# Router logits of a mixture-of-experts stage, with the tokens as the stationary operand

## The reference

```python
def _L3_ffn_ref(x, gate_w, w_gate, w_up, w_down, sw_gate, sw_up, sw_down):
    b, l, d = x.shape                                  # E, H, K = 16, 128, 8
    xf = x.reshape(-1, d)
    logits = _l2norm(xf) @ _l2norm(gate_w).T
    scores = jax.nn.sigmoid(logits)
    topk_scores, topk_idx = jax.lax.top_k(scores, K)
    topk_w = topk_scores / jnp.sum(topk_scores, axis=-1, keepdims=True)
    combine = jnp.sum(jax.nn.one_hot(topk_idx, E, dtype=xf.dtype) * topk_w[..., None], axis=1)
    g = jnp.einsum('nd,edh->neh', xf, w_gate)
    u = jnp.einsum('nd,edh->neh', xf, w_up)
    y = jnp.einsum('neh,ehd->ned', jax.nn.silu(g) * u, w_down)
    routed = jnp.einsum('ned,ne->nd', y, combine)
    shared = jax.nn.silu(xf @ sw_gate) * (xf @ sw_up) @ sw_down
    return (routed + shared).reshape(b, l, d)
...
x = x + jnp.tanh(g_ffn[3]) * _L3_ffn_ref(_layernorm(x, axis=-1), ...)
```

## Time and profile before

| | |
|---|---|
| times of three runs | 1162.62, 1164.57, 1879.65 us |
| median | 1164.57 us |
| time of the profiled execution | 1164.86 us |
| its span, first to last instruction | 1163.1 us |
| mean granted clock of PE | 0.963 |
| busy over the span | PE 1059.1 us (91%), DVE 796.5 (68%), ACT 517.9 (45%), POOL 165.6 (14%) |

### The profile page before, as it was taken

The page is one execution under the profiler, slowest core; times in us unless marked ns, Lnnn a source line. Parts: engine busy times, 40 slices in busy tenths (PEclk is TensorE's granted clock), DMA queues, the critical chain, the costliest instruction groups (busy, mean ns, idle before and its releaser), DMA issues.

```text
span 1163.1 us, 18686 instructions
## 1 busy us (share of the span) xinstructions
PE 1059.1 (91%) x6180; PEld 906.3 (78%) x6180; DVE 796.5 (68%) x1816; ACT 517.9 (45%) x1190; POOL 165.6 (14%) x224
## 2 busy tenths in 40 slices
PE   4775799998899969997999997999969999999998
PEld 3664467776899948886888886999848888888887
DVE  5597889976788745436888875888547564565544
ACT  2556544432555545444544452566533333333222
POOL 2231000000112043211111001133213000010000
PEclk9988899999999979998999998999979999999999
DMA  9301010001000000000000005000012212121221
GB/s 288 85 1 39 1 11 1 1 1 39 34 1 0 1 12 1 1 1 1 1 1 0 0 1 228 4 0 1 1 49 62 66 51 77 56 73 46 67 83 32
DMA packets 30373, 41.18 MB, mean 35 GB/s; under 512 B 13615, under 2 KB 19577, under 8 KB 29414
## 3 DMA queue, kind: packets, MB, share of 16 engines
q1 hardware_dynamic: 29437, 39.63, 11.1%
q10 hardware_dynamic: 873, 0.72, 0.3%
HBM read 37.80 MB, written 2.54 MB: 35 GB/s over the span
## 4 chain that ended last, share of the span: by engine, by line
PE 82%; DVE 9%; ACT 4%; issue 2%; DMA 2%; SPq 1%; POOL 1%; DVEq 0%; POOLq 0%; ACTq 0%
PE psum L1919 15%; PE psum L1929 8%; PE psum L1518 7%; PE psum L336 6%; PE psum L1328 6%; PE psum L1151 6%; PE psum L1109 5%; PE psum L1306 5%; PE psum L1732 4%; PE psum L1526 4%; PE psum L1719 3%; PE psum L1122 2%; PE psum L1133 2%; PE psum L1316 2%; PE psum L552 1%
## 5 line engine op out<-in xcount | busy, mean ns | idle before, releaser
L298 POOL TENSOR_TENSOR rstd<-ve,mhalf 128x1 f32<-128x1 f32 x128 | 81.3, 635 | 748.8 <-DVE ve L293 748.8
L347 ACT COPY work<-psum 128x256 f32<-128x256 f32 (+1 forms) x240 | 99.0, 437 | 148.4 <-PE psum L336 146.0
L336 PE MATMUL psum<-ident,work 128*128 128x128 f32 (+1 forms) x624 | 104.0, 291 | 33.1 <-DMA ctx<-in_ctx_r 8.9
L336 PEld LDWEIGHTS psum<-ident,work 128*128 128x128 f32 (+1 forms) x624 | 78.4, 151 | 48.0 <-issue 9.1
L2052 DVE TENSOR_TENSOR work<-psum,work 128x512 f32<-128x512 f32 x68 | 46.9, 690 | 88.3 <-ACT work L1989 88.1
L1992 ACT CAST h_hi<-work 128x512 fp32r<-128x512 f32 x68 | 42.2, 621 | 112.1 <-DVE work L2057 101.7
L1518 PE MATMUL psum<-early,work 128*128 128x352 f32 x256 | 84.1, 485 | 6.7 <-ACT zone L480 4.0
L1919 PE MATMUL psum<-x_hi,ew_hi 128*128 128x512 f32 (+1 forms) x272 | 87.1, 402 | 2.6 <-ACT work L1989 2.6
L1919 PE MATMUL psum<-x_lo,ew_hi 128*128 128x512 f32 (+1 forms) x272 | 85.2, 395 | 0.0
L1919 PE MATMUL psum<-x_hi,ew_lo 128*128 128x512 f32 (+1 forms) x272 | 84.6, 392 | 0.0
L1929 PE MATMUL psum<-ew_hi,h_hi 128*128 128x256 f32 x272 | 76.4, 281 | 4.7 <-DVE x L2072 3.8
(11 more groups left out here) (258 smaller groups left out, 2542.6 us busy)
## 6 DMA issues: line engine op xcount, KB each, us to landing
work<-expert_shares SPq DMA_DIRECT2D x64, 256.0 KB, 3.2
early<-in_experts_in SPq DMA_DIRECT2D x1, 6528.0 KB, 20.0
x<-in_x_in SPq DMA_DIRECT2D x4, 512.0 KB, 7.5
early<-in_W_in SPq DMA_DIRECT2D x2, 1024.0 KB, 6.0
out_x<-x SPq DMA_DIRECT2D x3, 512.0 KB, 4.4
early<-in_Wk SPq DMA_DIRECT2D x1, 1024.0 KB, 6.8
early<-in_Wq SPq DMA_DIRECT2D x1, 1024.0 KB, 9.1
zone<-in_Wv SPq DMA_DIRECT2D x1, 1024.0 KB, 13.6
```

What stands on the lines that cost most here:

```text
L298: pool.tensor_tensor(rstd[:, slot:slot + 1], ve[:, slot:slot + 1], mhalf[:, 0:1], ALU.pow).then_inc(s["rstd_ready"], 1)
L336: last = pe.transpose(dst[0:rows, at:at + n], src, ident[0:n, 0:n])
L347: act.copy(dst, src).then_inc(s["tr_copied"], 1)
```

## The change

The logits are made with the tokens as the stationary operand. For each of the group's four tiles, six products (three of the split times two halves of the width) load 128 columns of `x_hi` or `x_lo` and stream the 16 columns of `gw_hi` or `gw_lo`; the result has the tokens on the partitions, as the ranking wants it. So 24 products of 16 columns take the place of six of 512 columns, and the four transposes of logits, the copy to `lgT` and the tile `lgT` go. ACT copies the result to `lg` at unit 7 in place of unit 9. The first two gate/up units of the stage both stand behind the logits, at units 7 and 8. The count `tr` is six per group, and waits on it are renumbered. The loop over groups 1 and 2 is written out on PE; ACT and DVE keep theirs.

```diff
-        XT_AT, LG_AT, BT_AT, Z_AT, SIG_AT, TOP_AT, CT_AT = range(2, 6), 7, 9, 10, 10, 11, 13
+        XT_AT, LG_AT, Z_AT, SIG_AT, TOP_AT, CT_AT = range(2, 6), 7, 10, 10, 11, 13
+        FIRST_UNITS = (LG_AT, LG_AT + 1)
...
                 if e == LG_AT:
                     pe.wait_ge(s["tr_copied"], tr.n)
-                    cols = bass.ds(g1 * 512, 512)
-                    passes = [(w, a, k) for w, a in ((gw_hi, x_hi), (gw_hi, x_lo), (gw_lo, x_hi)) for k in range(KD)]
-                    for n, (w, a, k) in enumerate(passes):
-                        last = pe.matmul(bank[5][0:NE, :], w[:, k, :], a[:, k, cols], start=n == 0,
-                                         stop=n == len(passes) - 1)
-                    last.then_inc(s["tr_filled"], 1)
-                    tr.up()
-                if e == BT_AT:
-                    pe.wait_ge(s["tr_copied"], tr.n)
-                    settle(pe, tensor_waits_taken)
                     for j in range(GT):
-                        last = pe.transpose(bank[5][:, j * NE:(j + 1) * NE], lgT[:, j * P:(j + 1) * P],
-                                            ident[0:NE, 0:NE])
+                        cols = bass.ds((g1 * GT + j) * P, P)
+                        passes = [(a, w, k) for a, w in three((x_hi, x_lo), (gw_hi, gw_lo)) for k in range(KD)]
+                        for n, (a, w, k) in enumerate(passes):
+                            last = pe.matmul(bank[5][:, j * NE:(j + 1) * NE], a[:, k, cols], w[:, k, :],
+                                             start=j == 0 and n == 0, stop=j == GT - 1 and n == len(passes) - 1,
+                                             skip_group_check=True)
                     last.then_inc(s["tr_filled"], 1)
                     tr.up()
...
             for e in range(NU):
                 side(0, e)
-                if e in (LG_AT, BT_AT):
-                    gate_up(0, (LG_AT, BT_AT).index(e))
+                if e in FIRST_UNITS:
+                    gate_up(0, FIRST_UNITS.index(e))
             group(0, True, True)
-            looped(pe, [(tr, 7)], G - 2, lambda i: group(i + 1, True))
+            for g in range(1, G - 1):
+                group(g, True)
             group(G - 1, False)
...
                 if e == LG_AT:
-                    act.wait_ge(s["tr_filled"], tr.up())
-                    act.copy(lgT, bank[5][0:NE, :]).then_inc(s["tr_copied"], 1)
-                if e == BT_AT:
                     act.wait_ge(s["tr_filled"], tr.up())
                     act.copy(lg, bank[5][:, 0:GT * NE].rearrange("p (a b) -> p a b", a=GT)
                              ).then_inc(s["tr_copied"], 1)
...
-                    dve.wait_ge(s["tr_copied"], 7 * g1 + 6)
+                    dve.wait_ge(s["tr_copied"], 6 * g1 + 5)
...
-                sp.wait_ge(s["tr_copied"], 7 * g + 7)
+                sp.wait_ge(s["tr_copied"], 6 * g + 6)
```

More of the change, by code:

```diff
@@ L392, in flamingo @@
         share = [carve(work, at, (512,)) for _ in range(RING)]
-        lgT = carve(work, at, (512,), F32, NE)
         combT = carve(work, at, (512,), F32, NE)
@@ L2004, in moe_scalar @@
             group(0, True, True)
-            looped(act, [(tr, 7)], G - 2, lambda i: group(i + 1, True))
+            looped(act, [(tr, 6)], G - 2, lambda i: group(i + 1, True))
             group(G - 1, False)
```

## The result

| | before | changed |
|---|---|---|
| median of 6 runs each | 1164.40 us | 1170.11 us |
| lowest and highest | 1162.62 to 1879.65 | 1169.43 to 1173.55 |
| span of the profiled execution | 1163.1 | 1167.7 |
| products of PE in it | 6180 | 6236 |
| mean granted clock | 0.963 | 0.957 |

The ratio is 1.0055, 95% interval 1.0043 to 1.0067: slower by 5.7 us (some 5.0 to 7.8), clear of noise and far within two per cent. The forecast was 1172, from +7.3. The 1879.65 is a single run of the kernel before, 60% above all others of it, and does not enter the ratio.

What follows compares the result with a forecast made beforehand. The prediction took PE's queue to bound the stage's steady part and a chain of waits its start. From 1164.9 us it added 0 (loop), 2.6 (loads), 3.4 (clock) and 1.3 (start) to reach 1172, range 1164 to 1177.

Steps and rivals of the forecast that it cites:

- The written-out loop: PE's loop over groups 1 and 2: writing it out gains nothing, 0, bounds -0.3 and +1 us.
- The loads: Three steady groups: 24 short products cost more than the removed work, +0.86 us per group, +2.6 us (0.6 to 3.3).
- The restart of 0.10: Behind each steady burst: 0.1 us for restarting long products, whose first load has nothing to hide behind.
- the removed 1.92: Steady groups: old logits products (1.38) and their transposes (0.54) cost 1.92 us per group, all on the path.
- the transposes' 0.085: Old logits' transposes, 0.085 us each, taken as the lower bound of a short product's step: +0.2 us per group.
- The clock: Steady bursts: short products often drop PE's clock; two drops in three bursts taken, +3.4 us (0 to 10).
- The start: Start of the MoE stage: PE reaches the combine weights' transposes 1.0 to 1.4 us later, +1.3 us (-0.5 to +1.8).
- The sum: Whole kernel: 1164.9 + 0 + 2.6 + 3.4 + 1.3 = 1172.2 us; median 1172.
- Rival B: Steady bursts: the clock holds, so 1164.9 + 2.6 + 1.3 = 1168.8 us; chance 0.26.

Runs made afterwards that it cites:

- e5: Changed kernel with the combine weights' transposes at the start moved between the gate and up halves of the second unit; ratio 1.0034, median 1168.40 us.
- e4: Changed kernel with each of the 24 products streaming its 16 columns eight times over (128 columns); ratio 1.0029, median 1168.24 us.
- e8: Changed kernel with 128-column streaming and the combine weights' transposes between the halves of unit 1 at the start; ratio 1.0000, median 1166.39 us.
- e3: Changed kernel with each steady burst of 24 short products cut into four of 6 around the down products; ratio 1.0032, median 1167.77 us.
- e7: Changed kernel with each steady short product put behind one long product of units 7 and 8; ratio 1.0072, median 1172.83 us.
- e10: Changed kernel with each steady short product put behind one long product of units 8 and 9; one run, 1169.23 us.
- e9_old_earlier: Kernel before, loop written out, logits' transposes right behind the copy, combine weights' transposes directly behind unit 0, unit 1 behind them; ratio 1.0005, median 1164.08 us.
- e2_start_only: Kernel before with the loop written out and the 24 short products only in the first preparation; ratio 1.0008, median 1164.77 us.
- e6: Kernel before, loop written out, logits' transposes right behind the copy, combine weights' transposes between the halves of unit 1; ratio 0.9986, median 1163.07 us.

## Why the prediction was right, point by point

**The written-out loop, 0.** Right: 293.84 against 293.79 in the run with that alone.

**The loads, +2.6 in the steady part.** Measured 2.31 (the run with wide products, at full clock). The step was 0.1075 us rather than the 0.1116 of L563: per group 6.72 (889.08 to 895.80) - 4.14 = 2.58, against 2.68 + 0.10. The restart of 0.10 was right too: behind the second burst, where the clock held, the unit took 2.83 against 2.73. So 2.58 + 0.10 - 1.92 = 0.76 a group, 2.3 in three, and the removed 1.92 stands. The choice of L563 and L1109 over the transposes' 0.085 was right; that the load alone sets the step is shown by the wide products.

**The clock, +3.4.** Measured 3.31, from two drops in three bursts: the unit behind takes 4.42 and 4.44 against the 2.83 behind the burst without a drop, 1.6 each (1.7 forecast), and a little more on the products around it. That there were two was taken, not worked out, so the close agreement is partly luck; in the run e5 it was one. That short products with 128-column loads cause it is shown three ways: the same loads with more to stream (no drop), the same products cut up (no drop), twice the burst (three drops, each about twice as long). Over all traces, the clock fell at three of six bursts of 24 (changed kernel, e5), at three of three of 48, at none of six with wide products (e4, e8) and at none of nine places where the products were cut up or interleaved (e3, e7, e10). Why one burst of 24 drops it and another does not stays open. The Trainium skill's advice in "TensorE: Matmul & The Clock Gate", "Why this matters for your kernels", is to leave no long idle gaps between bursts of products. In e9_old_earlier the clock did fall behind a gap, though a shorter one (2.3 us) than the page warns of, and it held behind the same gap in e5 and e8; the drops at the bursts came with PE busy in every record. The measurement decides: a busy PE was not enough.

**The start, +1.3.** Measured +0.82 in the changed kernel, within the -0.5 to +1.8 given, and +1.98 in e2_start_only, a little over it. The mechanism is as forecast: the 24 products took 5.14 us at half clock (4.9 to 5.4), the combine weights were ready early, PE came late. The clock rose 2.7 us behind the first dense product in one and 5.3 in the other, both outside the 3.4 to 4.6 assumed, and that is the spread; the +1.3 lies between two values of which each trace shows one or the other. The forecast's count was also a little short: 4.6 us at 0.423 are eleven products, not ten, so PE would be free by 862.3.

**The sum.** 7.3 forecast, 6.44 in the stage of the profiled execution (0.82 + 5.62): the loads came 0.3 under the forecast, the clock 0.1 and the start 0.5. Between the medians it is 5.7, 5.0 to 7.8 by the interval. Part of the 0.7 between 6.44 and 5.7 may be executions with fewer drops or another clock at the start; the runs' times (1169.43 to 1173.55) and mean clocks (0.953 to 0.959) vary, and only one execution has a trace, so that stays open. Rival B, the clock holds (1168.8), is what e3 and e4 made real, at 1167.8 and 1168.2. The 25 ns or so that the same page of the Trainium skill gives under "Back-to-back issue gap" for a product of few columns was reached by none of these: 0.1075 is four times that, as every product here brings its own load of 128 columns, and by the wide products the load is what sets it.

## What to carry to other kernels

In a run of like products each cost the larger of its load and its stream (0.11 us with 16 or 128 columns streamed, 0.2275 with 512), so here the side with more columns belonged on the moving operand: turning the roles to save four tiny transposes replaced 1.92 us by 2.7. Long and short products in turn did not follow that: together they took 0.345. A run of products with little to stream can pull the clock down even if PE never idles; here it cost more than the loads themselves, and letting them stream more, or cutting the run up, took it away at next to no cost. And in an in-order queue at the head of a stage, look at what stands ahead of the one instruction that feeds the chain: moving it ahead of six products took 1.2 to 1.4 us off the start in the traces. Moving it further took off as much again, and in the one execution traced most of that was lost to a slower clock. None of the reordered kernels is shown by its times to be faster than the kernel before.

## What the runs showed of the hardware that I had not expected

- Streaming eight times as many columns beneath the same load cost 0.05 us for 24 products (2.63 against 2.58) and gave 3.31 us back through the clock.
- Idle time of one length did not fix the clock: behind 2.3 to 2.4 us without a product it was at 0.50 for 6.7 us in e9 and for some 3 us in e6, and held in e5 and e8. Behind the wait of 2.57 us ahead of the third gate/up unit of the stage it was at 0.50 within about 1 us in all nine traces that have that wait. The residual waits of up to 1.4 us inside the steady part were never followed by a drop.
- A long and a short product in turn cost 0.345 us, 0.117 more than the long one alone: a long product hid one load of 128 columns, but not two.
